# Routed experts of a fused two-layer model: each slot's token found by 0/1 products, token rows gathered tile by tile instead of scattered and loaded

## The reference, cut to what matters

```
def _L0_ffn_ref(x, up, gate, down, router, w_up_s, w_gate_s, w_down_s):
    x_ = x.reshape(b * t, c)                      # layer-normed residual, 1808 x 256
    idx = jnp.argmax(x_ @ router.T, axis=-1)      # one of 8 experts for each token
    onehot = jax.nn.one_hot(idx, router.shape[0], dtype=x.dtype)
    u = jnp.einsum('bc,ehc->ebh', x_, up)
    g = jnp.einsum('bc,ehc->ebh', x_, gate)
    ye = jnp.einsum('ebh,ech->ebc', jax.nn.silu(g) * u, down)
    y = jnp.einsum('ebc,be->bc', ye, onehot)
    ys = jax.nn.silu(x_ @ w_gate_s.T) * (x_ @ w_up_s.T) @ w_down_s.T    # the shared expert
    return (y + ys).reshape(b, t, c)
```

## Time and profile before

| | |
|---|---|
| median of three runs | 780.9 us (777.01, 780.9, 785.78) |
| the profiled execution's own time | 784.5 us |
| its span in the trace | 782.7 us |
| granted clock over the span | 0.954 of full |
| PE busy | 694.2 us, 89% of the span |
| DVE, ACT, POOL busy | 63%, 48%, 42% |

### The profile page before, as it was taken

One profiled execution on the slowest core, in us unless ns is written; L12 is line 12 of the kernel. 1 busy time (PEld: TensorE's weight loads), 2 busy tenths in 40 slices (PEclk: granted clock), 3 DMA queues, 4 the chain that ended last, 5 costly groups with the idle time before them and its releaser, 6 DMA issues. The chain is left out here.

```text
span 782.7 us, 11907 instructions
## 1 busy us (share of the span) xinstructions
PE 694.2 (89%) x3798; PEld 460.4 (59%) x3799; DVE 491.7 (63%) x885; ACT 375.0 (48%) x852; POOL 328.2 (42%) x310
## 2 busy tenths in 40 slices
PE   7799999998999789999996779898898897868986
PEld 5578888885666455666664646566565563423444
DVE  1656666666412115444126778898888988996786
ACT  0456666664211032333222676765756856211965
POOL 0011221110276313223221178878878878631436
PEclk9999999999999999999998899999999998979999
DMA  9993000000021261111104211202202202000003
GB/s 256 308 426 166 0 0 0 0 1 1 2 43 23 48 210 35 47 40 47 46 29 110 95 42 55 97 2 95 95 0 95 96 0 96 0 0 1 1 1 96
DMA packets 28838, 52.94 MB, mean 68 GB/s; under 512 B 10975, under 2 KB 23683, under 8 KB 26627
## 3 DMA queue, kind: packets, MB, share of 16 engines
q1 hardware_dynamic: 20067, 47.64, 17.9%
q0 software_dynamic: 8736, 4.85, 2.5%
HBM read 42.78 MB, written 9.60 MB: 67 GB/s over the span
## 5 line engine op out<-in xcount | busy, mean ns | idle before, releaser
L503 POOL TENSOR_TENSOR arena<-arena 128x904 f32<-128x904 f32 x64 | 124.9, 1952 | 66.4 <-DVE arena L1294 59.2
L1294 DVE TENSOR_TENSOR_SCAN arena<-ps,arena 128x452 f32<-128x452 f32 x128 | 133.6, 1086 | 11.6 <-POOL arena L503 4.5
L814 ACT ACTIVATE ps<-arena,sh_w 128x448 f32<-128x448 f32 x128 | 79.2, 632 | 94.8 <-DVE arena L1294 94.3
L1609 PE MATMUL ps<-arena,work 128*128 x176 | 83.9, 601 | 0.0
L578 ACT ACTIVATE work<-ps,work 113x113 f32<-113x113 f32 x256 | 66.5, 386 | 30.6 <-DVE work L948 30.6
L1284 DVE TENSOR_TENSOR arena<-arena,ps 128x904 f32<-128x904 f32 x64 | 69.0, 1078 | 12.6 <-PE ps L1789 12.4
L442 POOL TENSOR_TENSOR xT<-work 128x452 f32<-128x452 f32 x16 | 15.1, 942 | 139.2 <-DVE work L937 139.2
L551 POOL DMA_INDIRECT answers_e<-work,slot_token x22 | 23.6, 1073 | 97.7 <-DVE work L1089 97.7
L535 POOL DMA_INDIRECT slots_in<-xn,slot x16 | 37.8, 2365 | 51.8 <-issue 51.8
L1802 PE MATMUL ps<-arena,const 128*128 128x452 f32 x80 | 40.0, 583 | 21.2 <-POOL arena L507 21.1
L1807 PE MATMUL ps<-arena,const 128*128 128x452 f32 x96 | 47.6, 623 | 10.9 <-POOL arena L503 10.9
(11 more groups left out here) (254 smaller groups left out, 1369.6 us busy)
## 6 DMA issues: line engine op xcount, KB each, us to landing
arena<-c_rows SPq DMA_DIRECT2D x8, 1808.0 KB, 6.5
arena<-in_ex_w SPq DMA_DIRECT2D x8, 1536.0 KB, 22.5
slots_in<-work SPq DMA_DIRECT2D x1, 2827.0 KB, 22.9
work<-slots_in SPq DMA_DIRECT2D x22, 128.5 KB, 2.0
xn<-answers_e SPq DMA_DIRECT2D x4, 448.0 KB
out<-resid SPq DMA_DIRECT2D x8, 224.0 KB
arena<-in_patches SPq DMA_DIRECT2D x3, 576.0 KB, 6.3
sh_w<-in_sh_w SPq DMA_DIRECT2D x1, 1536.0 KB, 12.2
```

The costliest lines, as they stand in the source:

```text
L503: pool.tensor_tensor(read[kp], state[kp], c_all[par][:, 2 * c:2 * c + 2, :].unsqueeze(2).broadcast_to([P, 2, KT, N]), ALU.mult)\
L814: act.activation(decay_ps(n)[:, :, 1:], delta[par].rearrange("p k (b s) -> p (k b) s", b=GB)[:, :, 1:], ACT.Exp, scale=a_neg[:, 2 * c + n: ...
L1294: dve.tensor_tensor_scan(state[kp][:, n].rearrange("p k s -> p (k s)"), decay_ps(n).rearrange("p q s -> p (q s)"), drive[kp][:, n].rearran ...
L1609: last = pe.matmul(ps[:, bank, :], xgT[par][:, k, :], arena[:, bass.ds(e * EW + at + k * HID, HID)], start=k == 0, stop=k == KT - 1)
```

## The change

It finds the inverse map, slot to token, on chip, and gathers rows by it.

- DVE compares each token's slot with the tiles' first slots (`tile_from`, `tile_hot`) and with the 128 places (`place_hot`, 0/1 in bf16). `named_hot` is the tile's 0/1 row times the token's row number plus one, and times its sequence number. Sixteen products on PE, summed over the sequences, give for each place and tile both numbers; DVE makes of them `slot_token` (where the answer goes) and `gather_token` (which row to fetch).
- The normed rows are stored once, in token order, to `rows_in` in DRAM by SP. POOL gathers each tile by an indirect transfer into a place of its own: tiles 0 to 5 in the space of `guq`, 6 to 17 in that of `xn2`, 18 in `work`, 19 to 21 in that of `dq`. It issues the first 18 before the experts' answers, at most four in flight.
- Gone: the filler write, the 16 scatters, the 22 tile loads, `keep_tokens`, two small copies.
- The gate and up weights of the quantised block come as one load of four blocks and eight loads of one block, each of these when the gathered tile in its place has been transposed.
- On PE the loop over groups 1 and 2 and the loop over tiles 4 to 15 are written out.

```
-            sp.wait_ge(pool_set, 1)
-            sp.wait_ge(cast_done, 4 + KT + 2)
-            sp.dma_start(slots_in.rearrange("(t p) d -> p t d", p=P),
-                         zero.unsqueeze(1).broadcast_to([P, ETILES, D + 1])).then_inc(slots_zeroed, 16)
...
-            sp.wait_ge(scattered, 16 * B)
...
+            for n in range(B // 4):
+                sp.wait_ge(xn2_ready, 4 * n + 4)
+                theirs = rows_in[4 * n * S:4 * (n + 1) * S].rearrange("(b s) d -> s b d", s=S)
+                for rows in (slice(0, SROWS), slice(SROWS, S)):
+                    sp.dma_start(theirs[rows], xn2[rows, 4 * n:4 * n + 4, :]).then_inc(rows_out, 16)
+            sp.wait_ge(rows_out, 16 * (B // 2))
+            sp.wait_ge(xn2T_ps, B)
+            sp.dma_start(raw_gu[:, 0:FREE_RAW, :], a["f_gate"][:, 0:FREE_RAW, :]).then_inc(ffn_in, 16)
...
+            for w in range(FREE_RAW, 2 * FT):
+                sp.wait_ge(xgT_ps, IN_GUQ + w - FREE_RAW + 1)
+                sp.wait_ge(ffn_in, 16 * (w - FREE_RAW + 1))
+                sp.dma_start(raw_gu[:, w, :], a[("f_gate", "f_up")[w // FT]][:, w % FT, :]).then_inc(ffn_in, 16)
...
+            def gather(j):
+                pool.indirect_dma_start(xg(j), None, rows_in, bass.IndirectOffsetOnAxis(ap=gather_token[:, j:j + 1], axis=0))\
+                    .then_inc(xg_in[j % IN_FLIGHT], 16)
+            def landed(j):
+                pool.wait_ge(xg_in[j % IN_FLIGHT], 16 * (j // IN_FLIGHT) + 16)
+                pool.sem_inc(xg_ready, 1)
+            pool.wait_ge(rows_out, 16 * (B // 2))
+            pool.wait_ge(xn2T_ps, B)
+            pool.wait_ge(slots_ready, 2)
+            for j in range(GATHERED_FIRST):
+                gather(j)
+                if j >= IN_FLIGHT - 1:
+                    landed(j - IN_FLIGHT + 1)
...
+        def dve_map(dve, q):
+            q.step(dve.tensor_tensor(tile_from, slotf.unsqueeze(2).broadcast_to([S, B, ETILES + 1]),
+                                     const[0:S, C_FIRST:C_FIRST + ETILES + 1].unsqueeze(1).broadcast_to([S, B, ETILES + 1]), ALU.is_ge))
+            q.done(dve.tensor_tensor(tile_hot, tile_from[:, :, 0:ETILES], tile_from[:, :, 1:ETILES + 1], ALU.subtract))
+            q.step(dve.tensor_reduce(tile_at, tile_from[:, :, 1:ETILES + 1], AX.X, ALU.add))
+            q.step(dve.scalar_tensor_tensor(out=place_at, in0=tile_at.rearrange("p b o -> p (b o)"), scalar=-float(ETILE), in1=slotf,
+                                            op0=ALU.mult, op1=ALU.add))
+            dve.tensor_tensor(place_hot, const[0:S, C_PLACE:C_PLACE + ETILE].unsqueeze(1).broadcast_to([S, B, ETILE]),
+                              place_at.unsqueeze(2).broadcast_to([S, B, ETILE]), ALU.is_equal).then_inc(chosen_ready, 1)
+            dve.tensor_scalar(named_hot[:, :, 0, :], tile_hot, const[0:S, C_ROW:C_ROW + 1], None, ALU.mult).then_inc(chosen_ready, 1)
+            dve.tensor_tensor(named_hot[:, :, 1, :], tile_hot, const[0:S, C_SEQ:C_SEQ + B].unsqueeze(2).broadcast_to([S, B, ETILES]),
+                              ALU.mult).then_inc(chosen_ready, 1)
...
+        def pe_find_tokens(pe):
+            pe.wait_ge(chosen_ready, 4)
+            for b in range(B):
+                last = pe.matmul(ps[:, 2, 0:2 * ETILES], place_hot[:, b, :], named_hot[:, b, :, :].rearrange("p n h -> p (n h)"),
+                                 start=b == 0, stop=b == B - 1)
+            last.then_inc(counts_ps, 1)
...
-            def turn(j, par, half):
-                pe.wait_ge(xg_in[par], half)
+            def turn(j):
+                pe.wait_ge(xg_ready, j + 1)
```

More of the change, by code:

```diff
@@ L220, in build @@
         onesb = sb("onesb", [S, S], BF16)
-        slot = sb("slot", [S, B], I32)
         tile_expert = sb("tile_expert", [1, ETILES], I32)
-        xg_named = [pl.take((D + 1,)) for _ in range(2)]
-        xg = [t[:, 0:D] for t in xg_named]
+        xg_work = pl.take((D,))
+        at_map = pl.at
         xgT = [pl.take((KT, ETILE)) for _ in range(2)]
@@ L1066, in group @@
                     if route and m == 3:
-                        dve_slots(dve)
+                        q = dve_slots(dve)
+                    if q is not None and not route and m == 2:
+                        dve_slot_tokens(dve, q)
                     par = m % 2
@@ L1104, in step @@
                 if weights:
+                    if loaded is not None:
+                        dve.wait_ge(ffn_in, loaded)
                     dve_weights(dve, j - 2, par)
-            with dve.Fori(1, 1 + FT) as i:
+            with dve.Fori(1, 1 + FREE_RAW // 2) as i:
                 for par in range(2):
                     step(2 * i + par, par, 16 * i, True)
+            with dve.Fori(1 + FREE_RAW // 2, 1 + FT) as i:
+                for par in range(2):
+                    step(2 * i + par, par, 16 * i, True, 32 * i + 16 * par - 16 * (FREE_RAW))
             for j in range(2 + 2 * FT, ETILES - 2):
@@ L1636, in pe_experts, with step @@
             pe.wait_ge(sresid_ready, 8 + 2)
-            def step(j, par, loaded, weights):
+            def step(j, par, weights):
                 e_down = gate_up(j + 1, 1 - par, j)
-                turn(j + 2, par, loaded)
+                turn(j + 2)
                 down(j, e_down)
```

165 lines of the change are left out of this document (86 added, 79 removed).

## The result

The kernel after takes 776.98 us in the median of 20 runs (771.05 to 779.97), the kernel before 782.3 us in the median of 20 (777.01 to 786.15). The medians lie 5.3 us apart; the ratio that weighs all the runs is 0.9944, with a 95% interval of 0.9923 to 0.9965: 4.4 us less (2.7 to 6.0). That is a real gain, and within 1%. The forecast was 775.4 us, 5.5 us less than before, in a range of 768.5 to 783.0. The profiled execution took 778.68 us.

What follows compares the result with a forecast made beforehand. PE was taken to bound the kernel, busy 694.2 of 782.7 us. The hole's -6.98, the products' +1.2 and the start's +0.3 summed to -5.5 us, from the 780.9 median to 775.4 us, range 768.5 to 783.0.

Steps and rivals of the forecast that it cites:

- The hole: PE's wait before the routed experts' first transposes: 5.05 us go, and 1.93 us of slow clock after it, minus 6.98 us.
- nothing else is late next: Before tile 0's gate products: weights landed long before, ACT's copies run under PE's down products, so the whole 6.98 us come.
- the last state-space load: The load of `a_log`, issued when the shared expert's down products end: it moves forward with everything else, time effect nothing.
- The sixteen products: New chain on PE in group 1, no hole beside it: plus 1.2 us (0.5 to 2.2).
- The map: DVE's inverse map takes 5.4 us, ends about 214.8, one microsecond before PE asks: nothing (0 to plus 1.0).
- POOL and SP: Scatters and loads removed, gathers, stores and single weight loads added, on engines PE did not wait for: nothing (0 to plus 1).
- the rival of the held-back answers: Eighteen gathers on POOL delay the first answer's scatter; decides from 4.0 us a gather, 795 us, chance 5%.
- a_log: ACT's wait for this load in step 0, then PE's: nothing; to minus 2.3 us or plus 1 by the clock.
- the second hole: Rival at the state-space loads: `a_log` lands earlier, ACT waits less, PE's clock does not fall; -9.8 us, 771.1, chance 14%.
- Start: At the kernel's start, 88 KB more constants stand ahead of the text: plus 0.3 us; from below, minus 0.5.
- The sum: Over the whole kernel: -6.98 + 1.2 + 0.3 = -5.5 us, from 780.9 to 775.4 us.
- the near row: For POOL's gathers, the answers' scatter of 128 rows of 256 numbers: 1.076 us on POOL, 2.5 us to landing.

Runs made afterwards that it cites:

- Experiment 9: Kernel after, with the product that makes the map's 2048 columns done three times: 781.25 us, ratio 0.9998 to the kernel before.
- Experiment 1: Kernel before, with the first two tiles' transposes reading other data so that PE does not wait for the first loads: 781.26 us, ratio 0.9986.
- experiment 10: Kernel after, with one gather in flight instead of four: 778.98 us, ratio 0.9958 to the kernel before.
- experiment 12: Kernel before, with 173 more columns of constants (88 KB) in the load at the start, read by nothing: 781.93 us, ratio 1.001.
- experiments 5 to 7: `a_log` loaded first of the state-space loads: on the kernel after 772.3 us; on the kernel before 778.43 us; on the kernel before with 128-row scatters 770.43 us.
- experiment 5: Kernel after, with `a_log` loaded ahead of the other state-space loads and ACT waiting for it alone: 772.3 us, ratio 0.9875 to the kernel before.
- experiment 3: Kernel before, with 128 rows a scatter in place of 113, fifteen spare rows a block going behind the table: 775.53 us, ratio 0.9917.

## Why the prediction was right, point by point

*The hole goes, with the half clock behind it:* -6.98 forecast, -7.34 in the trace. Shown; 0.2 of the 0.36 us come from the four transposes and eight products, which took 269.97 - 267.80 = 2.17 us and not 2.37. Experiment 9 shows the same trade the other way round, 2.90 us of waiting for 4.3 us of time. But the argument that nothing else is late next held only because the change also moves what feeds PE. Experiment 1, which removes this wait and nothing else, gains nothing that could be told. The prediction says of the last state-space load that "it moves forward with everything else" (it did, by 7.9 us, from 285.39 to 277.48); without that half there is no gain, and it deserved a rival of its own.

*The sixteen products:* +1.2 us forecast, 0.41 measured, outside 0.5 to 2.2. The step that was mis-sized is the choice of the two bf16 transposes at 0.055 us as the nearest row; the other row of the group, 31 ns for a product with a quarter of the weights, was near the 26 ns measured, and what was added for filling and draining the array did not show. The Trainium skill ("TensorE: Matmul & The Clock Gate", "Part 2: What happens when you issue a matmul") gives about 62 ns a matmul where the decoding is not done in hardware; the 26 ns of this trace do not show such a floor.

*The map:* nothing forecast, none found. It ended at 213.29 instead of 214.8, and two thirds of that is only that it began at 208.48 instead of 209.44, in an execution that was ahead by about as much on PE too. It took 4.81 us instead of 5.4: the large operation cost what the line through two rows had it or more (2.29 us for 2048 columns, 2.23 forecast), those of 352 columns 0.40 to 0.53, and the 0.3 us put between them did not come. So the cover was 1.66 us instead of 1.0.

*POOL and SP:* nothing forecast, none found. The gathers behave as the answers' scatters did, 1.26 us each against the 4.0 at which the rival of the held-back answers decides. But the prediction also has it that even one at a time would be under that point: experiment 10 shows 4.04 us in the mean, since each gather waits for the landing of the one before, 3.2 us in the median from issue. The estimate of 2.3 us was too low.

*`a_log`:* nothing forecast, 0.5 us gained in the pair of profiles, within the bounds given. It is not a steady gain: where the kernel after or a variant keeps this order, PE's wait was 2.28, 2.55, 3.50 and 4.49 us, in the kernel before and in experiment 12 it was 2.78 and 2.79. (The bound of -2.3 us took 4.5 us as spent at half clock; at the mean of 0.62 of its own row it was 4.5 x 0.38 = 1.7, and in the kernel after the slow products cost 1.8.) That the second hole goes as well did not happen; the argument against it, the transfers directly ahead in the same queue, was right, as experiments 5 to 7 show by moving the load to their front.

*Start:* +0.3 forecast, not told from zero by experiment 12.

*The end of the span:* not in the prediction, +1.1 us, in every profile of the kernel after and its variants.

*The sum:* -7.34 + 0.41 + 0.3 - 0.5 + 1.1 = -6.0 by the measured sizes (the 0.3 of the start being the forecast's own), and -4.4 (2.7 to 6.0) by the ratio. So the two just touch. That the forecast of -5.5 comes so near is in part luck: the hole was put 0.4 too small, the products 0.8 too dear and `a_log` at nothing for 0.5, and these three made up for the end's 1.1 us, which had no term. The level of 775.4 us was off for a second reason: the three runs it starts from have a median of 780.9, the twenty 782.3. What takes back the remaining 1.6 us, if anything does, stays open; the uneven wait for `a_log` could, and experiment 5, which removes it, gained 5.4 us where the one trace had 4.2. Of the fourteen profiles, the low clock between 30 and 50 us was in three, all of the kernel before or variants of it; the half clock in the last block was in two, the kernel after and that of experiment 3.

*What the prediction did not ask* is why the scatters were slow. It read 2.36 us and 8.4 us beside 1.08 and 2.5 for nearly the same bytes and took the near row for the gathers, rightly, "since size and row count are the same". Which of the two it was mattered: changing the row count is enough, and experiment 3 has the whole gain of the change at least (6.5 us against 4.4, intervals overlapping) without the map, the products or the gathers. The Trainium skill, "DMA: Bandwidth & Descriptors", section "Why a DMA increments its semaphore by 16 and not by 1", says that a transfer is dealt out to the largest number of engines up to 16 that divides the slowest dimension: by that 113, a prime, goes to one engine, 120 to fifteen, 128 to sixteen. (It excepts some direct copies on this chip, and does not name indirect transfers.) The traces agree in which counts fall together: 113 alone, 120 and 128 alike. They do not show how many engines moved a scatter, and one engine alone does not fit easily. By the shares above the packets of a scatter of 113 rows took 0.176 x 16 x 63 / 16 = 11.1 us, more than its 8.4 us from issue to landing, and those of a scatter of one number 0.388 x 48.73 = 18.9 us against 5.2; with 128 rows it is 0.229 x 26 = 6.0 against 2.6. Unless the times of packets overlap on an engine, several engines took part in each. So that the row count sets the price is shown; why it does is open.

## What to carry to other kernels

When an indirect transfer costs twice what its neighbour does, compare their numbers of rows before rebuilding what depends on it: seven or fifteen spare rows did what a new way of finding tokens did. When a stall is taken from the engine that bounds the kernel, look at the queue whose transfers it waits for next, and try the removal alone: here it was worth nothing until the queue was early too. And put a small load that somebody waits for ahead of the large ones that nobody does; that was worth 3.0 to 5.4 us in the three versions where it was tried by itself.

## What the runs showed that was not expected

Indirect scatters of 113 rows hold POOL for 2.35 us whatever a row's length, 257 numbers or one, and POOL halts after eight of them, for 8.7 to 9.9 us with long rows and 3.40 us with one number; scatters and gathers of 120 or 128 rows hold it for 0.94 to 1.16 us, the case below aside, and do not halt. Sixteen bf16 products of 44 columns with full weights take 26 ns each. The span of the kernel after goes on for 1.9 us behind its last transfer, that before for 0.8.

And what POOL has under way or begins beside one cast of 2.28 us on DVE is held up until about the cast's end. In the kernel after that is a gather's issue, 2.71 us in place of 1.0:

```profile
290.53 2.71 POOL L545 DMA_INDIRECT dq<-rows_in,gather_token  x1 [0.30 <-issue]
...
290.84 2.28 DVE L1294 CAST xT<-const 96x4096 bf16<-96x4096 f32 x1
```

In the kernel before it is a cast of a single column, 2.13 us in place of 0.18:

```profile
299.43 2.28 DVE L1247 CAST xT<-const 96x4096 bf16<-96x4096 f32 x1
...
299.63 2.13 POOL L544 CAST slot_token<-apart 128x1 int32<-128x1 f32 x1
```

It is so in all fourteen profiles: the POOL cast in the nine of the kernel before and its variants, the gather in four of the others, and in experiment 10 the first scatter of an answer (2.48 us, above), which fell beside the DVE cast there. It follows the cast wherever it falls; the cast was not moved on purpose. In the kernel after PE did not wait behind it.
